# Query and key weights first: the head of a fused attention and expert kernel put in another order

## The reference

```
x = x + w_o( softmax( mask( q k^T ) / sqrt(1024) ) v )      q, k, v = w_q, w_k, w_v of layernorm(x), each 1024 wide
x = x + ffn(layernorm(x))                                    ffn: 8 experts, the best 2 of a token, SwiGLU 128 -> 256 -> 128
```

## Time and profile before

| | |
|---|---|
| median of three runs (lowest to highest) | 240.25 us (239.41 to 241.43) |
| the profiled execution, its own time | 239.77 us |
| its span in the trace | 238.0 us |
| PE busy (instructions) | 227.5 us, 96% of the span (1814) |
| DVE busy | 185.9 us, 78% |
| POOL busy | 162.1 us, 68% |
| ACT busy | 145.8 us, 61% |
| chain that ended last | PE 79%, POOL 6%, DMA 4%, issue 3%, DVE 3%, ACT 2% |

### The profile page before, as it was taken

How to read it: one execution, slowest core, us unless ns; L and a number is a source line. 1 busy time by engine, 2 the same in 40 slices (tenths; PEclk the granted TensorE clock), 3 DMA queues, 4 the chain that set the end, 5 groups by cost and what they waited for, 6 DMA issues and landing times.

```text
span 238.0 us, 6499 instructions
## 1 busy us (share of the span) xinstructions
PE 227.5 (96%) x1814; PEld 209.2 (88%) x1815; DVE 185.9 (78%) x848; ACT 145.8 (61%) x391; POOL 162.1 (68%) x204
## 2 busy tenths in 40 slices
PE   7989999999999999999999999989999999999973
PEld 6978888898799767877999999979999999999973
DVE  2479898879897789977898799757666666699955
ACT  2267787777877757755599665646565656565200
POOL 6513327888888888868577777777777777777500
PEclk9999999999999999999999999999999999999999
DMA  6999800111111111115134426533433434598474
GB/s 229 310 321 332 226 4 28 43 37 45 34 50 35 48 34 47 45 37 136 37 70 107 114 82 145 137 92 101 105 112 91 106 95 108 183 342 266 121 266 134
DMA packets 31947, 28.89 MB, mean 121 GB/s; under 512 B 4137, under 2 KB 26545, under 8 KB 31921
## 3 DMA queue, kind: packets, MB, share of 16 engines
q1 hardware_dynamic: 26448, 19.39, 29.7%
q0 software_dynamic: 4096, 8.53, 10.6%
q10 hardware_dynamic: 1376, 0.66, 1.0%
HBM read 16.34 MB, written 12.22 MB: 120 GB/s over the span
## 4 chain that ended last, share of the span: by engine, by line
PE 79%; POOL 6%; DMA 4%; issue 3%; DVE 3%; ACT 2%; POOLq 1%; DVEq 0%; SPq 0%
PE scores L727 12%; PE turned L727 12%; PE scores L598 12%; PE weighed L654 11%; PE scores L748 6%; PE turned L624 5%; POOL expert_rows L505 4%; PE mixed L748 3%; PE weighed L748 3%; PE mixed L613 3%; PE mixed L612 3%; DMA XX<-choice_rows 2%; DVE X L1369 2%; PE scores L744 2%; DMA TL<-L_attn_w_o 1%
## 5 line engine op out<-in xcount | busy, mean ns | idle before, releaser
L505 POOL DMA_INDIRECT expert_rows<-rows,slots x64 | 64.5, 1008 | 18.2 <-issue 12.6
L516 POOL DMA_INDIRECT choice_rows<-ysb,ycol x64 | 63.6, 993 | 19.5 <-issue 10.7
L865 ACT ACTIVATE Wt<-W 128x512 f32 x71 | 44.1, 624 | 15.7 <-issue 15.7
L727 PE MATMUL scores<-xT,Wt 128*128 128x128 f32 x288 | 38.3, 276 | 1.1 <-issue 1.1
L598 PE MATMUL scores<-XX,TL 128*128 128x512 f32 (+3 forms) x96 | 38.1, 506 | 0.2 <-ACT TL L838 0.2
L654 PE MATMUL weighed<-TL,PT 128*128 128x136 f32 x272 | 37.0, 281 | 0.8 <-DVE X L989 0.7
L727 PE MATMUL turned<-xT,Wt 128*128 128x128 f32 x280 | 37.1, 275 | 0.0
L727 PEld LDWEIGHTS scores<-xT,Wt 128*128 128x128 f32 x288 | 35.0, 192 | 1.4 <-issue 1.4
L654 PEld LDWEIGHTS weighed<-TL,PT 128*128 128x128 f32 x272 | 33.7, 190 | 1.7 <-issue 1.6
L727 PEld LDWEIGHTS turned<-xT,Wt 128*128 128x128 f32 x280 | 34.1, 192 | 0.0
L977 DVE TENSOR_REDUCE negmax<-scores 128x1 f32<-128x128 f32 (+7 forms) x32 | 23.5, 734 | 4.9 <-PE scores L598 4.9
(11 more groups left out here) (182 smaller groups left out, 462.6 us busy)
## 6 DMA issues: line engine op xcount, KB each, us to landing
xt<-expert_rows SPq DMA_DIRECT2D x71, 66.0 KB
XX<-choice_rows SPq DMA_DIRECT2D x16, 256.0 KB, 4.0
W<-L_ffn_w SPq DMA_DIRECT2D x2, 1024.0 KB, 9.6
out<-X SPq DMA_DIRECT2D x9, 128.0 KB
X<-L_attn_in_features SPq DMA_DIRECT2D x2, 512.0 KB, 7.6
expert_rows<-rows,slots POOLq DMA_INDIRECT x64, 2.5
choice_rows<-ysb,ycol POOLq DMA_INDIRECT x64, 2.3
out<-X ACTq DMA_DIRECT2D x5, 128.0 KB
```

The lines of the kernel that those rows point to most:

```text
L505: nc.gpsimd.indirect_dma_start(xs, bass.IndirectOffsetOnAxis(ap=slots[:, u, k:k + 1], axis=0), rows[:, u % ROWS_RING, k, :], None).then_in ...
L516: nc.gpsimd.indirect_dma_start(yb, bass.IndirectOffsetOnAxis(ap=ycol[:, q, 0:1].bitcast(u32), axis=0), ysb[:, q, :], None).then_inc(y_out[ ...
L727: mm(bank[2 + j % RING][:, c * P:(c + 1) * P], Wt[:, j % RING, c * P:(c + 1) * P], xT[:, j % RING, :], start=True, stop=True)
L865: copy(Wt[:, j % RING, :], W[:, ds(w * (SET // WIDE), SET)], ACT.Copy).then_inc(Wt_rdy, 1)
```

## The change

**SP.** The first four tiles of x are issued first, then w_q and w_k, then w_o and w_v. The load of the third sequence gets a semaphore of its own.

**PE.** A is made first. The query projections of tiles 0 to 3 (`query`, 128 columns) come apart from their values (`values`, 144 columns). The turns of w_o, the scores of tiles 0 and 1, M, the turns of the probabilities of tiles 0 and 1, the turn of M, MG and the scores of tile 2 follow, and then the values of tiles 0 to 3 in one go. The loop starts with slot 2. One product of the identity is added in front (`WARM` 6) and the eight of `WARM_ON` are gone.

**ACT.** For tiles 0 to 3 it copies the query (128 columns), and later the values (136 columns) and the logits (8 columns) by instructions of their own. The copy of tile 4's transpose stands behind all of them.

**DVE and POOL.** `STAT1_EARLY` goes from 12 to 10, so the statistics of the first layer norm run two tiles less ahead and `rstd_1` stands in slots 5, 9, 13, 17 and 21, with one for tiles 8 to 11 in slot 1, ahead of all scatters. `woT` and `MT` move from `PT` to `Wt`.

```
-STAT1_GROUP, STAT1_EARLY = 4, 12
-WARM, WARM_ON = 5, 8
+STAT1_GROUP, STAT1_EARLY = 4, 10
+WARM = 6
+AHEAD_Q = 4
...
-            sp.dma_start(wo_sb, w_o).then_inc(wo_in, 16)
...
-            sp.dma_start(wv_sb, w_v.rearrange("(p c) i -> p c i", p=P)).then_inc(wv_in, 16)
...
+            sp.dma_start(wo_sb, w_o).then_inc(wo_in, 16)
+            sp.dma_start(wv_sb, w_v.rearrange("(p c) i -> p c i", p=P)).then_inc(wv_in, 16)
...
+            def query(u):
+
+                pe.wait_ge(xx_ev, u + 1)
+                wait(pe, tl_ev, u - 1)
+                mm(early_query(u), A_sb[:, :], XX[:, token_tile(u), :], start=True, stop=True).then_inc(tl_mm, 1)
+
+            def values(u):
+
+                mm(early_values(u), XX[:, token_tile(u), :], M_sb[:, :], start=True, stop=True).then_inc(v_mm, 1)
...
+            transposes(1 - XT_LEAD)
+            pe.wait_ge(A_rdy, 1)
+            query(0)
+            transposes(2 - XT_LEAD)
+            query(1)
             pe.wait_ge(wo_in, 16)
...
-            for _ in range(WARM_ON):
-                mm(pM[:, 0:P], identf[:, :], identf[:, :], start=True, stop=True)
+            pe.wait_ge(consts, N_CONST)
+            scores(0)
+            query(2)
+            transposes(3 - XT_LEAD)
+            scores(1)
+            query(3)
             pe.wait_ge(wv_in, 16)
+            pe.wait_ge(gwT_rdy, 1)
...
+            turn(0)
+            pe.wait_ge(M_rdy, 1)
+            nc.tensor.transpose(pO[:, P:2 * P], M_sb[:, 0:P], identf[:, :]).then_inc(MT_mm, 1)
+            turn(1)
             pe.wait_ge(MT_rdy, 1)
             mm(pO[:, 0:E], MT, M_sb[:, VG:], start=True, stop=True).then_inc(MG_mm, 1)
-            transposes(1 - XT_LEAD)
-            pe.wait_ge(A_rdy, 1)
+            scores(2)
+            pe.wait_ge(tl_ev, AHEAD_Q)
             pe.wait_ge(MG_rdy, 1)
-            pe.wait_ge(consts, N_CONST)
+            for u in range(AHEAD_Q):
+                values(u)
+            transposes(1)
+            weigh(0)
...
+            def out_query(u):
+                act.wait_ge(tl_mm, u + 1)
+                copy(TL[:, token_tile(u), 0:P], early_query(u), ACT.Copy).then_inc(tl_ev, 1)
+
+            def out_values(u):
+                act.wait_ge(v_mm, u // 2 * 2 + 2)
+                copy(TL[:, token_tile(u), P:], early_values(u)[:, 0:VG], ACT.Copy).then_inc(v_ev, 1)
+                act.wait_ge(sd1_rdy, 1)
+                copy(X[:, token_tile(u), D:], early_values(u)[:, VG:], ACT.Copy, scale=sd1[:, u:u + 1]).then_inc(xg_rdy, 1)
...
+            exps(2)
+            for u in range(AHEAD_Q):
+                out_values(u)
+            out_xx(1)
```

More of the change, by code:

```diff
@@ L529, in await_rows @@
                 waiting.extend((gr, v, k) for v in range(a, a + n) for k in range(K))
-            for s in range(N_TILES):
+            for s in range(2, N_TILES):
                 u = s + STAT1_EARLY
@@ L774, in step @@
                     ranks(group_at(N_TILES + j, RANK_LAG))
-            projections(-TV_LEAD)
-            projections(1 - TV_LEAD)
-            for s in range(2 - XT_LEAD, N_TILES):
+            for s in range(2, N_TILES):
                 if has_xx(s):
@@ L782, in _ @@
                     scores(s + S_LEAD)
-                if s > 1 - TV_LEAD and has_tl(s):
+                if has_tl(s):
                     projections(s)
-                if is_tile(s):
-                    turn(s)
-                if is_tile(s - PV_LAG):
-                    weigh(s - PV_LAG)
+                turn(s)
+                weigh(s - PV_LAG)
                 if group_at(s, RANK_LAG) is not None:
@@ L875, in exp_logits @@
                 copy(elog[:, a:a + n, :], dlog[:, a:a + n, :], ACT.Exp).then_inc(elog_rdy, 1)
-            for s in range(-XT_LEAD, LAST_SLOT + 1):
+            out_xx(-XT_LEAD)
+            act.wait_ge(A_mm, 1)
+            copy(A_sb[:, :], pS[0][:, 512:512 + P], ACT.Copy, scale=float(F_ATT) ** -0.5).then_inc(A_rdy, 1)
+            out_xx(1 - XT_LEAD)
+            out_query(0)
+            out_xx(2 - XT_LEAD)
+            out_query(1)
+            act.wait_ge(woT_mm, FC)
+            copy(woT[:, FC // 2:, :].rearrange("p c q -> p (c q)"), pT[1][:, :], ACT.Copy).then_inc(woT_hi_rdy, 1)
+            out_query(2)
+            exps(0)
+            out_xx(3 - XT_LEAD)
+            out_query(3)
+            exps(1)
+            act.wait_ge(M_mm, 1)
+            copy(M_sb[:, 0:P], pO[:, 2 * P:3 * P], ACT.Copy).then_inc(M_rdy, 1)
+            out_pt(0)
+            act.wait_ge(MT_mm, 1)
+            copy(MT, pO[:, P:2 * P], ACT.Copy).then_inc(MT_rdy, 1)
+            out_pt(1)
+            exps(2)
+            for u in range(AHEAD_Q):
+                out_values(u)
+            out_xx(1)
+            for s in range(2, LAST_SLOT + 1):
                 if s == N_TILES:
```

102 lines of the change are left out of this document (44 added, 58 removed).

## The result

| | before | after |
|---|---|---|
| median, range, in us (4 runs each, same chip) | 240.84, 239.41 to 241.63 | 245.00, 243.57 to 245.76 |
| ratio after to before, 95% interval | | 1.0195, 1.0153 to 1.0236 |
| profiled execution, its span | 239.77, 238.0 | 243.57, 241.8 |
| PE's first instruction of slot 2 | 18.08 | 21.60 |
| from there to the same instruction of slot 24 (transpose of tile 27) | 70.42 | 71.11 |

The change makes the kernel slower by a ratio of 1.0195, 4.2 us between the medians; 241.8 us and at most 243.4 were forecast. Ratios are given as recorded with their 95% intervals; the quotient of the medians beside them can differ by up to 0.4% (here it is 1.0173). They leave out executions in a slower state of the chip, of which there are none here, three of the eight of e7_no_warm_on and one of the ten of e6_idle.

What follows compares the result with a forecast made beforehand. The prediction took PE to bound the kernel, so that delaying its entry into the loop delays everything behind. Median 240.25 us plus 1.6 (1.1 for the head, 0.5 for POOL) gave 241.8 us, range 240.3 to 243.4.

Steps and rivals of the forecast that it cites:

- 1.1 for the head: Work ahead of slot 2: slot 2 starts at 19.2 us against 18.08, a loss of 1.1 us.
- 0.5 for POOL: Loop: a fourth `rstd_1` behind the first scatter costs PE 0.5 us, out of 0 to 1.2.
- The loads: Head: x lands at 3.5 us, the halves of q and k at 5.9 and 7.5, w_o 8.7, w_v 9.9.
- step 2: A in the head: starts at 5.95 us, full rate from 6.8, result at 8.6; the sixth identity product costs nothing.
- named as a rival: Head: PE's clock rises late, delaying by 0.75 or 1.7 us; 242.5 to 243.5 us in all, chance 0.20.
- steps 3 to 6: Head behind A: copies, w_o turns, scores, M, values, then late ACT copies, bringing slot 2 to 19.2 us.
- the sign named in advance: DVE's longest wait for `rstd_2` in slots 21 to 23; PE's waits for DVE, 60 to 118 us, grow half a microsecond.
- The rival in which PE pays all of 1.24 us: Loop: POOL's added inverse root delays PE in full; 242.6 us in all, chance 0.15.
- the part that was to come back at the first scatter: Slot 7: the first scatter loses the `rstd_1` of its own slot, giving back part of POOL's cost; no separate size.
- The rival in which the PE order pays: Head: without a late ACT path slot 2 starts at 15.5 us; 238 to 239 us in all, chance 0.06.
- The fast loads: Head: q and k move as fast as w_v, landing at 4.7 and 5.9 us; 240.9 us in all, chance 0.11.
- that of the range: Whole kernel: from 240.3 us (fast loads, with the runs' scatter) to 243.4 us (late clock).

Runs made afterwards that it cites:

- e7_no_warm_on: Kernel before without the eight identity products of `WARM_ON`, nothing else changed: 240.57 us against 239.69, ratio 1.0019.
- e6_idle: Kernel before without the eight identity products, PE also waiting for w_v before it turns w_o: 242.56 us, ratio 1.0115.
- e2_stat12: Kernel after with the first layer norm's statistics again 12 tiles ahead (tiles 12 and 13 before slot 2): 269.48 us on a 266 us chip, ratio 1.0158.
- e1_warm: Kernel after with four more identity products while PE waits for the weights of A: 268.11 us against 266.32, ratio 1.0102.
- a_again: Kernel after, unchanged, traced again on another chip: 244.84 us against 240.21 for the kernel before, ratio 1.0187.
- e3_tile4: Kernel after with tile 4's transpose ahead of the values and its copy ahead of tile 2's exponentials: 267.78 us against 266.32, ratio 1.0049.
- e5_warm_tile4: Kernel after with both e1_warm and e3_tile4: 241.74 us against 240.21, ratio 1.0062.
- b_again: Kernel before, unchanged, traced again on another chip: one run of 240.95 us; the kernel before has 240.21 there over 19 runs.
- e9_before_stat10: Kernel before with `STAT1_EARLY` 10 in place of 12 and the guards that follow from it: 240.12 us, ratio 1.0026.

## Why the prediction was wrong

The sum was 1.1 for the head and 0.5 for POOL. The head measured 3.52, POOL's part 0.69, the end -0.41. By its own steps:

**The loads: too optimistic.** x and the layer norm came as predicted (x at 3.7, `xn` of tile 0 from 6.2). The halves of q and k came at 6.7 and 8.33 against 5.9 and 7.5 (7.55 in the steps). The scatter is wide (the first half at 5.95 to 6.7 in the traces with four loads, the second at 7.4 to 8.6), and this one lay at its late end.

**Rate of A (step 2): the step that failed.** "The sixth identity product costs nothing: PE waits for weights there" counted that wait as free and took over the rise at 6.8 us from a head that has no such wait. What it cost can be read from e2_stat12, which has the same order at full rate: slot 2 stands 19.84 - 7.77 = 12.07 us behind the landing of the second half of the weights. In after it is 21.60 - 8.33 = 13.27, so the late clock cost 1.2 us in this trace; e1_warm, read in the same way (19.69 - 7.57 = 12.12), says 1.15. In a_again, where the turns of w_o are slow too, it is 23.12 - 8.41 = 14.71, a cost of 2.6 us, and e6_idle makes the loss in the old kernel. It was named as a rival, and in the first trace with the right price (0.75 to 1.7 us), but with a chance of 0.20. The argument against it, that PE had been idle for 0.3 us at 4.05 in the old head and the rise came on time, misread the rows. PE of before in order of time has the turn of the router weights between the two that were read:

```profile
3.99 0.27 PE L680 MATMUL weighed<-identf,gwc 8*128 8x8 f32 x1
4.36 1.97 PE L684 MATMUL turned<-identf,TL 128*128 128x128 f32 x8
```

PE was idle for 0.10 us there, and that was compared with more than 1.2. It said nothing of long stretches.

**The serial path (steps 3 to 6): right in its course, 0.42 us too short.** From the landing of the second half of the weights to slot 2 the prediction has 19.2 - 7.55 = 11.65 us; at full rate the trace of e2_stat12 has 12.07. The turns of w_o took 0.88 us (0.9 predicted), the idle time ahead of query 3 was 0.23 (0.4), and the end is the one described, ACT of after in order of time, to set beside the earlier trace rows:

```profile
19.38 0.58 ACT L889 ACTIVATE Pr<-scores,negmax 128x384 f32<-128x384 f32 x1 [1.52 <-DVE negmax L1024]
...
19.95 0.27 ACT L873 ACTIVATE TL<-mixed 128x136 f32<-128x136 f32 x1
20.11 0.27 ACT L875 ACTIVATE X<-mixed,sd 128x8 f32<-128x8 f32 x1
...
21.21 0.34 ACT L852 ACTIVATE XX<-scores 128x128 f32<-128x128 f32 x1
```

The four pairs take 21.21 - 19.95 = 1.26 us (1.35 predicted), and PE's transpose of tile 5 waits for the copy behind them. e3_tile4 and e5_warm_tile4 show that 0.9 us of it is a matter of order alone.

So the head's 3.52 us are 1.12 as predicted, 0.78 for weights at 8.33 and not 7.55, 1.20 for the clock, and 0.42 for the serial path. In the median execution of after, 1.4 us slower than this one, more is lost; a_again suggests the clock, but of the other six executions no trace is kept.

**POOL: right, somewhat small.** 0.69 against 0.5 us. DVE and PE at slot 22 of after, DVE in order of time, then PE's waits from 60 to 120 us; they answer to the earlier trace rows:

```profile
88.66 0.47 DVE L1057 TENSOR_SCALAR rows<-X,mv,rstd 128x256 f32<-128x256 f32 x1 [1.52 <-POOL rstd L456]
```

```profile
PE mixed L617 <- DVE picked L1103: 1.1, 1, 1.1
...
PE weighed L659 <- DVE X L1036: 0.3, 1, 0.3
```

DVE waits 1.52 us where it waited 0.47, and what it makes for the routing comes later: PE's waits for DVE are 1.4 us against 0.9 (0.5 in b_again). That was the sign named in advance, at the place named in advance. On POOL the cause stands ahead of it, to set beside the earlier trace rows:

```profile
84.54 1.16 POOL L511 DMA_INDIRECT expert_rows<-rows,slots  x1 [0.20 <-ACT PT L883]
85.73 1.05 POOL L452 TENSOR_TENSOR rstd<-ve,halves 128x4 f32<-128x4 f32 x1
86.97 1.03 POOL L511 DMA_INDIRECT expert_rows<-rows,slots  x1 [0.20 <-issue]
88.04 0.58 POOL L456 TENSOR_TENSOR rstd<-ve,halves 128x1 f32<-128x1 f32 x1
```

The rival in which PE pays all of 1.24 us is refuted by the 0.69, and the part that was to come back at the first scatter is not seen there: it stands 18.7 us behind slot 2 in both kernels (40.27 and 36.76 us).

**What was not in the sum:** the 0.41 us behind slot 24. They lie within the scatter of one kernel: this part takes 149.50 us in before and 150.42 in b_again, and PE's longest wait for DVE in it is 1.4 and 2.4 us there, 1.0 and 2.4 in after and a_again. Without this luck the trace would have shown 4.2 us. The rival in which the PE order pays is refuted: even with A at full rate slot 2 never came before 19.6 us in the order of after, nor before 18.6 with the repair of e3_tile4, against 17.6 to 18.3 in before, b_again and e9_before_stat10. The fast loads did not occur: in the traces with four loads the halves came at 5.95 and 7.43 at the earliest, not at 4.7 and 5.9.

The remaining step was that of the range. With a chance of 0.20 on the clock and 0.15 on POOL taken as alternatives, the range ended at 243.4. They were not alternatives: the clock's loss, the head's own 1.1 and POOL's part are at different places, and their sum, 240.25 + 1.1 + 0.5 + 1.7 = 243.55, lay already outside.

Not settled: how often after gets its clock early (in the eight runs of it none is below 243.57 us, so seldom), why the q and k loads are slow, and whether the second wait within A costs anything on average. No version was shown to be faster than the kernel before.

## What to carry to other kernels

An idle stretch of TensorE in a kernel's first microseconds is not free, even where nothing else waits there: price it with everything that runs behind it until the clock is back, and fill it with products that compute nothing if the weights cannot come sooner. Here a late clock cost 1.2 and 2.6 us where A was slow (after, a_again) and 1.6 us where M was (e6_idle); in e7_no_warm_on it ate up the microsecond that leaving the filling out should have brought, so that the total looked unchanged. Compare two traces from the landing of a load on, so that a load that came sooner is not booked as a faster engine. And a layer norm moved by two slots can make the kernel slower 80 us later: look for the place at which the engine has no idle time left, and add the costs of places that do not exclude each other.
